# Moving eight merge groups into the mixed pass, one-hots of layer 2 by matmul, maxima turned four groups at a time

## The reference

```
# layer 0: two graph attention convolutions on the edges (src, dst)
xl, xr = x @ Wl + bl, x @ Wr + br
logits = einsum(leaky_relu(xl[src] + xr[dst]), att)      # 8 heads of 16, then 1 head of 64
m = segment_max(logits, dst);  ex = exp(logits - m[dst])
out = segment_sum(xl[src] * ex / segment_sum(ex, dst)[dst], dst) + bias
# layer 1: xw = h @ W ; out = segment_sum(norm * xw[src], dst), then layer norm
# layer 2: pos = h[src] + edge_attr ; segment_sum(gelu(pos @ W1) * bases, dst), two batch norms
# layer 3: three convolutions as in layer 1, each on the result of the one before
```

## Time and profile before

| | |
|---|---|
| median of 3 runs | 6667.94 us (6659.76 to 6667.99) |
| the profiled execution's own time | 6665.56 us |
| its span, first to last instruction | 6663.1 us |
| `gat_sums` of layer 1, of layer 2 | 478 us, 411 us |
| mixed pass | 459 us |
| busy TensorE, VectorE, ScalarE, GpSimd | 4832.1, 4076.8, 2301.7, 4523.2 us |

### The profile page before, as it was taken

How to read it: one execution, slowest core, us unless ns; L and a number is a source line. 1 busy time by engine, 2 the same in 40 slices (tenths; PEclk the granted TensorE clock), 3 DMA queues, 4 the chain that set the end, 5 groups by cost and what they waited for, 6 DMA issues and landing times. The chain is left out here.

```text
span 6663.1 us, 98108 instructions
## 1 busy us (share of the span) xinstructions
PE 4832.1 (73%) x22735; PEld 3486.0 (52%) x22735; DVE 4076.8 (61%) x13068; ACT 2301.7 (35%) x5676; POOL 4523.2 (68%) x4354
## 2 busy tenths in 40 slices
PE   3677775347776666544886996666666799999999
PEld 2344443236664444333776995555555455555555
DVE  7998985589976766335887445444444644344343
ACT  4344444369943333334994003222222400000000
POOL 1777777678867777777887661777777177276473
PEclk8555555579965555556997998877777799999999
DMA  5988865556644444333444884655555299899998
GB/s 202 296 300 289 280 192 148 133 101 142 140 81 108 105 108 102 81 80 57 76 76 127 286 289 135 185 159 160 159 161 153 75 303 305 290 305 300 307 305 258
DMA packets 915215, 1226.12 MB, mean 184 GB/s; under 512 B 248092, under 2 KB 652720, under 8 KB 901674
## 3 DMA queue, kind: packets, MB, share of 16 engines
q1 hardware_dynamic: 593614, 879.21, 41.2%
q0 software_dynamic: 206208, 217.12, 16.7%
q10 hardware_dynamic: 114828, 123.48, 5.6%
HBM read 981.30 MB, written 239.21 MB: 183 GB/s over the span
## 5 line engine op out<-in xcount | busy, mean ns | idle before, releaser
L1180 POOL DMA_INDIRECT ACC<-table,TABS x1760 | 1665.4, 946 | 623.1 <-issue 623.1
L1495 POOL DMA_INDIRECT BUF<-table,TABS x840 | 796.3, 948 | 589.1 <-issue 245.7
L1261 POOL DMA_INDIRECT adjacency<-TABS x600 | 962.8, 1605 | 251.2 <-issue 221.8
L1801 POOL DMA_INDIRECT TABS<-table,SPOT_SRC x836 | 789.1, 944 | 317.9 <-issue 317.9
L1983 PE MATMUL picked<-BUF,G 128*128 x2368 | 595.4, 433 | 445.8 <-DVE ACC L2008 401.3
L1983 PEld LDWEIGHTS picked<-BUF,G 128*128 128x128 f32 x2368 | 525.6, 327 | 687.3 <-issue 687.3
L2379 PE MATMUL asum<-BUF 128*128 128x144 f32 x3520 | 561.0, 305 | 165.7 <-DVE BUF L2357 162.7
L1991 DVE TENSOR_TENSOR picked<-picked,ACC 128x512 f32<-128x512 f32 (+1 forms) x440 | 247.7, 563 | 573.4 <-DMA ACC<-table,TABS 517.0
L1824 PE MATMUL pre<-wmat,BUF 128*128 128x128 f32 x1672 | 320.7, 352 | 370.5 <-DVE BUF L1850 357.6
L2379 PEld LDWEIGHTS asum<-BUF 128*128 128x128 f32 x3520 | 476.2, 197 | 196.7 <-issue 186.3
L2325 ACT ACTIVATE BUF<-iota_row,TABS 128x128 f32<-128x128 f32 x1760 | 555.1, 386 | 22.5 <-PEq L98 22.5
(11 more groups left out here) (449 smaller groups left out, 9763.6 us busy)
## 6 DMA issues: line engine op xcount, KB each, us to landing
TABS<-adjacency SPq DMA_DIRECT2D x272, 512.0 KB
BUF<-in_edge_pair SPq DMA_DIRECT2D x836, 128.0 KB
BUF<-adjacency SPq DMA_DIRECT2D x102, 1024.0 KB
BUF<-adjacency SPq DMA_DIRECT2D x204, 512.0 KB
adjacency<-zeros ACTq DMA_DIRECT2D x44, 1792.0 KB
G<-adjacency SPq DMA_DIRECT2D x136, 512.0 KB
kept<-ACC SPq DMA_DIRECT2D x220, 272.0 KB, 3.8
G<-kept SPq DMA_DIRECT2D x220, 272.0 KB
```

Of the source, the lines that this page charges most:

```text
L1180: po.indirect_dma_start(rows[:, slot, j, 0:width], None, tab, bass.IndirectOffsetOnAxis(ap=SRC[:, q * GT + j:q * GT + j + 1], axis=0)).the ...
L1261: po.indirect_dma_start(adj_flat, bass.IndirectOffsetOnAxis(ap=PLACE[:, k:k + 1], axis=0), TOTAL[:, k:k + 1], None, compute_op=ALU.add).th ...
L1495: po.indirect_dma_start(R[:, q % deep_ring, j, :], None, table, bass.IndirectOffsetOnAxis(ap=SRC[:, k:k + 1], axis=0)).then_inc(S(f"gather ...
L1801: po.indirect_dma_start(R[:, g % RD, j, :], None, table, bass.IndirectOffsetOnAxis(ap=SPOT_SRC[:, k:k + 1], axis=0)).then_inc(S(f"gathered ...
```

## The change

Three things are changed. **Merges:** the last 8 far groups become a segment of their own and are merged inside the mixed pass, after the gathers of its first four near groups; beside `gat_sums` of layer 2 there are 46 groups in place of 54. Only 142 groups are waited for before the pass, and each chunk's first load waits, by a table `NEED`, for 142 or for all 150. The near groups move to units 18 + 1.2 q. **Layer 2's one-hots:** in place of four Abs on ScalarE, SyncE fetches bit codes of the group and TensorE multiplies them by a constant (`meet`), so that one Relu from PSUM gives the one-hots. At the fourth group TensorE runs 8 extra matmuls of 384 columns whose result is not used. **Maxima,** both layers: one fetch per head and one turn for four groups.

```diff
+RUN_UP, RUN_UP_LONG = 3, 8
+IN_MIXED = 8
+HALVES = ((0, FIRST_FAR), (FIRST_FAR, FAR))
+SEGMENTS = ((0, FIRST_FAR), (FIRST_FAR, FAR - IN_MIXED), (FAR - IN_MIXED, FAR))
-MERGES = ((1, 11, 61, 7), (1, 4, 54, 11))
+MERGES = ((1, 11, 61, 7), (1, 4, 46, 11))
...
-        def merge_rest():
-            merge(FAR)
+        def merge_up_to(groups):
+            merge(groups - sent[0])
             for s in merged:
-                po.wait_ge(s, 16 * GT * FAR // 2)
+                po.wait_ge(s, 16 * GT * groups // 2)
...
-            places = near_by(6, 1.3)
+            places = near_by(18, 1.2)
...
                 def load_units():
-                    for s in merged:
-                        sp.wait_ge(s, 16 * GT * FAR // 2)
                     for n, (c, w, b, deep) in enumerate(units):
+                        if b == 0:
+                            need = nc.values_load(NEED[0:1, c:c + 1], engines=(SP,), ...)
+                            for s in merged:
+                                sp.wait_ge(s, need)
...
                     for q in range(NEAR):
+                        if q == RING:
+                            merge_up_to(FAR)
                         wait(po, S("near_summed"), q - RING + 1)
...
                 def turn_max(q, slot, turn):
+                    if slot:
+                        return
+                    pe.wait_ge(S(f"max{turn % 2}"), 16 * H * (turn // 2 + 1))
+                    wait(pe, S("mfirst"), RING * (turn - 1))
+                    pe.matmul(mcol[turn % 2][:, 0:RING * TH], MX[:, turn % 2, :], ident[0:RING * TH, 0:RING * TH],
+                              start=True, stop=True).then_inc(S("mcol"), 1)
...
+                def meet(q, slot, turn):
+                    if not by_codes:
+                        return
+                    pe.wait_ge(S(f"codes{q % CD}"), 16 * (q // CD + 1))
+                    wait(pe, S("hot"), q - 1)
+                    pe.matmul(meets[slot % 2][:, :, :].rearrange("p t d -> p (t d)"), coded[:, q % CD, :],
+                              COLUMNS[0:CODE_ROWS, :, :].rearrange("p t d -> p (t d)"), start=True, stop=True
+                              ).then_inc(S("met"), 1)
...
                 def exps(q, slot, turn):
                     ac.activation(RHS[:, slot, :, W:W + H], DIF[:, slot], ACT.Exp).then_inc(S("exp"), 1)
+                    if by_codes:
+                        ac.wait_ge(S("met"), q + 1)
+                        wait(ac, S("summed"), q - RING + 1)
+                        ac.activation(HOT[:, slot], meets[slot % 2][:, :, :], ACT.Relu).then_inc(S("hot"), 1)
+                        return
...
+                    if by_codes and q == RUN_UP:
+                        for _ in range(RUN_UP_LONG):
+                            pe.matmul(mcol[0][:, P:4 * P], ident[:, :], X[:, 0:3, :].rearrange("p b d -> p (b d)"),
+                                      start=True, stop=True)
```

More of the change, by code:

```diff
@@ L1240, in clashes @@
             go(ve, lambda: ve.tensor_tensor(CLEAR[:, :], CLEAR[:, :], CLASH[:, :], ALU.add))
+            first_of_last, needs = st[4][0:1, 304:305], st[4][0:1, 320:320 + DENSE]
+            go(ve, lambda: ve.tensor_copy(first_of_last, blocks[:, FAR - IN_MIXED:FAR - IN_MIXED + 1, 0]))
+            go(ve, lambda: ve.tensor_scalar(needs, iota_row[0:1, 0:DENSE], float(CB), float(LIGHT + CB - 1),
+                                            ALU.mult, ALU.add))
+            go(ve, lambda: ve.tensor_scalar(needs, needs, first_of_last, float(16 * GT * IN_MIXED // 2),
+                                            ALU.is_ge, ALU.mult))
+            go(ve, lambda: ve.tensor_scalar(NEED[:, :], needs, float(16 * GT * (FAR - IN_MIXED) // 2), None, ALU.add))
             given_f, wrap = st[4][0:1, 200:200 + CYCLE], st[4][0:1, 256:256 + CYCLE]
@@ L1299, in load_units @@
                 def load_units():
-                    for s in merged:
-                        sp.wait_ge(s, 16 * GT * FAR // 2)
                     for n, (c, w, b, deep) in enumerate(units):
+                        if b == 0:
+                            need = nc.values_load(NEED[0:1, c:c + 1], engines=(SP,),
+                                                  min_val=16 * GT * (FAR - IN_MIXED) // 2, max_val=16 * GT * FAR // 2)
+                            for s in merged:
+                                sp.wait_ge(s, need)
                         wait(sp, S("used"), n - len(RA) + 1)
@@ L1940, in gat_logits @@
             assert len(OHT) == HD
-            own = range(NEAR + SEGMENTS[half][0], NEAR + SEGMENTS[half][1])
+            own = range(NEAR + HALVES[half][0], NEAR + HALVES[half][1])
             by_group = head_d[0:H * TILES * P].rearrange("(h g t e) -> g t h e", h=H, t=GT, e=P)
@@ L2084, in put_aside @@
                     done = 2
-                    middle = (own[0] + own[-1] + 1) // 2
-                    for s, e, i in ((own[0], middle, 0), (middle, own[-1] + 1, 1)):
+                    parts = [(NEAR + s, NEAR + e) for s, e in SEGMENTS if HALVES[half][0] <= s < HALVES[half][1]]
+                    for s, e, i in [part for s, e in parts for part in ((s, (s + e) // 2, 0), ((s + e) // 2, e, 1))]:
                         ve.copy_predicated(PLACE[:, s * GT:e * GT].rearrange("p (g t) -> p g t", t=GT),
@@ L2131, in gat_logits @@
                               (store_rows, ROWS_LATE + 1)])
-                po.wait_ge(S("aside"), 4)
+                po.wait_ge(S("aside"), 2 + 2 * len([s for s, _ in SEGMENTS if HALVES[half][0] <= s < HALVES[half][1]]))
                 po.wait_ge(filled, 16 * (len(UNIT_LIST) + 1 + HEAVY))
@@ L2284, in gat_sums @@
             at += RING * GT
-            MX = BUF[2][0:TH, at:at + RING, :]
+            MX = BUF[2][0:RING * TH, at:at + 2, :]
             DIF = BUF[2][:, at + RING:at + 2 * RING, 0:TH].rearrange("p r (t h) -> p r t h", h=H)
-            by_group = head_d[0:H * TILES * P].rearrange("(h g t e) -> g t h e", h=H, t=GT, e=P)
+            of_four = head_d[0:H * TILES * P].rearrange("(h n k e) -> n h k e", h=H, k=RING * GT, e=P)
             whole, R, LOGIT = ring(W, H)
+            by_codes = H == 1
+            coded = CODES[:, :, :].rearrange("p r e -> p (r e)")[0:CODE_ROWS, 0:CD * P].rearrange(
+                "p (r e) -> p r e", r=CD)
             with ExitStack() as ps:
+                meets = [psum(ps, f"meets{i}", [P, GT, P]) for i in range(2)]
                 mcol = [psum(ps, f"mcol{i}", [P, 4 * P]) for i in range(2)]
@@ L2294, in fetch_max @@
                 def fetch_max(q, slot, turn):
-                    wait(sp, S("mcol"), q - RING + 1)
+                    if slot:
+                        return
+                    wait(sp, S("mcol"), turn - 1)
                     settle(sp, "sync")
[L2298 to L2302, removed]
+                    for h in range(H):
+                        sp.dma_start(MX[h * RING * GT:(h + 1) * RING * GT, turn % 2, :], of_four[turn, h]
+                                     ).then_inc(S(f"max{turn % 2}"), 16)
                 def fetch_rows(q, slot, turn):
@@ L2311, in turn_max, with max_of, fetch_codes @@
                 def turn_max(q, slot, turn):
[L2312 to L2315, removed]
+                    if slot:
+                        return
[3 more added lines that the diff above has]
+                              start=True, stop=True).then_inc(S("mcol"), 1)
+                def max_of(slot, turn):
+                    return mcol[turn % 2][:, 0:RING * TH].rearrange("p (h r t) -> p r t h", h=H, r=RING)[:, slot]
                 def by_head(a):
                     return a.rearrange("p (t h) -> p t h", h=H)
+                def fetch_codes(q, slot, turn):
+                    if not by_codes:
+                        return
+                    wait(sp, S("met"), q - CD + 1)
+                    settle(sp, "sync")
+                    sp.dma_start(coded[:, q % CD, :], code_d[q * GT:(q + 1) * GT].rearrange("t b e -> (t b) e")
+                                 ).then_inc(S(f"codes{q % CD}"), 16)
+                def meet(q, slot, turn):
+                    if not by_codes:
+                        return
+                    pe.wait_ge(S(f"codes{q % CD}"), 16 * (q // CD + 1))
[3 more added lines that the diff above has]
+                              ).then_inc(S("met"), 1)
                 def hots(q, slot, turn):
+                    if by_codes:
+                        return
                     wait(ac, S("summed"), q - RING + 1)
```

15 lines of the change are left out of this document (9 added, 6 removed).

## The result

The changed kernel takes 6726.0 us against 6668.0 (median of four runs each); the ratio is 1.0093, 95% interval 1.0081 to 1.0106. The forecast was 6679, its range ended at 6708: the sign that had the most chance, and too small a size.

A forecast was written before the change was run, and what follows sets the result against it. It took VectorE to bound layer 1's sums, ScalarE layer 2's sums and TensorE the mixed pass. Terms -5, -7.6 and +25.7 gave +13 on 6665.6, 6678.6, stated as 6679 us; range 6636 to 6708.

The forecast's parts named there:

- part 1: Layer 1's sums: fewer turns of maxima save time only at the half clock level; ends -8 and +18, taken as -5 us.
- rival 3: Mixed pass: landings are slow beside loads, 13 us each, holding GpSimd's queue; +30, total 6705; chance 0.12.
- rival 4: Layer 1's sums: with less work TensorE's clock falls oftener, +18 in place of -5, total 6702; chance 0.10.
- The gain of the fewer turns (-7): Layer 1's sums: 17 groups at the half clock level each lose 0.35 us instead of 0.77, together -7 us.
- GpSimd's end caps it at 8: Layer 1's sums: the gain can't exceed 8 us, from GpSimd's merges ending at 1873.9 to VectorE's end at 1882.1.
- Part 2: Layer 2's sums: faster groups -15.6 us, run-up +6.5, first groups +1.5, sum -7.6.
- VectorE's chain at 1.753: Layer 2's sums: VectorE's chain of adds is the next limit, 1.753 us a group against 1.825, -15.6 us.
- Part 3: Mixed pass: stall before near group 4, half-level clock behind it and a wait before the last chunk; sum +25.7 us.
- The smaller handovers' -2: Mixed pass: handovers between chunks get shorter because near adds no longer lie in the way, -2 us.
- rival 1: Mixed pass: the merges hide there, total 6661; decides if GpSimd is back at gathers by 3701; chance 0.16.
- Rivals 2: Layer 2's sums: VectorE's floor is under 1.753 us, decided below 1.66 a group; total 6629, halfway 6650; chance 0.14.
- rival 5: Layer 2's sums: the new one-hots change nothing because ScalarE still paces; +8 there, total 6695; chance 0.04.

The follow-up runs named there:

- spread fetches: Changed kernel, but layer 1's maxima fetched for two of eight heads at each group's step, one turn of four groups earlier: 6693.1 us, ratio 1.0030.
- the kernel with its own maxima: Changed kernel, but layer 1's maxima fetched and turned as in the kernel before, four transfers and one turn in each group: 6696.5 us, ratio 1.0034.
- the copy left out: Kernel with spread fetches, without layer 2's weight column copy on VectorE from the fifth group on (wrong result): 6686.2 us, ratio 1.0029.
- with four groups: Kernel with spread fetches, ready blocks finished behind the last chunk but one's sum, four merge groups in the mixed pass, 50 in layer 2's sums: 6665.8 us, ratio 0.9996.

## Why the prediction was wrong

**The step that failed** is in part 1: "The maxima are the only thing changed. At the full clock VectorE bounds, and TensorE's turn is off its path: 0." It follows the edit through TensorE and stops there. The same edit turns four transfers a group into eight in every fourth, and they pass through SyncE's queue ahead of the rows that VectorE needs. No term stood there; measured, it is 42 to 49 us (482.5 and 477.8 against 524.3 and 526.5). With it, the sum is 6679 + 47 + 5, for the gain that no run shows: 6731, against 6726. The numbers were to be had: the kernel before issues four such transfers in 1.28 us, so that eight take more than a group's 2.01 by its own trace. (Two slips of the sum are small beside it: it names 2.4 us between the profiled execution and the median and leaves them out, 6681 with them, and rival 3's 6705 should be 6709.)

**The clock** (rival 4) was forecast as a cause of +18. The clock did fall, to 0.86, just above the 0.85 that I had named as the mark. The runs with spread fetches (0.95, the stage as short as before) and with more matmuls (0.97, the stage as long as in the change) reject it. The gain of the fewer turns (-7) is shown by nothing: the kernel with its own maxima has VectorE ready as early as the one with spread fetches (467.9 and 468.5 us, before 477.3). And the cap "GpSimd's end caps it at 8" took the merges' end for that of the kernel before: it comes 5 to 11 us later in the nine kernels without a burst of eight, for a reason that stays open, and 2 to 3 us lie between it and the end of the stage.

**Part 2** came out: 1.748 us a group for 1.753, ScalarE at 38% of the stage (152 of 403 us), -8.4 for -7.6. The run-up cost VectorE a wait of 7.1 (forecast 6.5), and that nothing is bought by it is shown by the two pairs with and without (404.4 and 397.2, 400.4 and 395.0). Right by its number and not by its reason is "VectorE's chain at 1.753": the copy left out shows that the period isn't the sum of VectorE's instructions. As the cause is open, the close fit may be luck. The median from group to group is 1.71 with the copy and without it, and longer steps now and then make the 1.75. GpSimd's merges end 60 us early. TensorE comes nearest: it is busy 271.6 of the same 300 us, 1.59 a group, so that its instructions and one short wait could be the whole period. What sets it stays open; neither this nor VectorE's own queue, which also loads each group's four addresses, was tried.

**Part 3** came out in its parts, 6 us too small in all: the stall 17.4 (16), landings 2.7, 5.3 and 2.4 (3 each), the half level behind the stall about 1.7 (2.5): 1.02 on the near products and 0.7 on the two units after them (8.03 for 7.31, as such pairs take elsewhere in the pass). The wait before the last chunk is 10.7 (10.1), released by the add that was named. The smaller handovers' -2 showed as well: all waits for line 1360's adds are 17.5 us, 10.7 of them the last one, where they were 9.7 with 0.9 for the last, so that the others fell from 8.8 to 6.8. Two short waits for gathers (2.5) were put at "a microsecond". These make 17.4 + 2.5 + 1.7 + 7.8 = 29.4 of the 31.7; where the rest lies was not looked for. The merges (rival 1) did not hide, and landings (rival 3) weren't slow. Rival 1's own point of decision was right: with four groups GpSimd is back at the gathers 30 us earlier and the stall is gone.

**Rivals 2 and 5**: neither (the mark of 1.66 us was not reached); but rival 5's core, that the one-hots by themselves give nothing, is what the run with 54 groups shows, by the merges' end and not by ScalarE.

## What to carry to other kernels

When small transfers are gathered into fewer steps, count their issues on the engine that issues them and look at what stands behind them in its queue: eight in a row at 0.45 us cost this stage 42 to 49 us, where eight spread over four groups were free. A clock below full in one stage can be the mark of a TensorE that waits; before it is called the cause, give TensorE more to do and see if the time moves. And an edit that frees one engine is worth nothing until the next limit in line, here the merges and the 6.7 us behind the last of them, is moved with it, and moved only as far as there is room.

## What the runs showed of the hardware

In a row, transfers of 4 KB (8 rows) cost SyncE 0.32 us each to issue, those of 8 KB (16 rows) 0.41 to 0.45, and a single one of 64 KB (128 rows) 0.37: the price hangs on the issue far more than on the bytes. A fetch of rows that had to wait behind such issues landed as fast after its own issue as any other (2.81 and 2.85 us). A stage whose last work is merges on GpSimd ended 6.7 us behind the last one in layer 2's sums and 2.7 us in layer 1's. And taking 0.20 of 1.75 us from the engine that seemed to set a loop's period gave back 0.02.
